# A Mamba layer and a mixture of experts on one core: softplus from exp and ln in one table set, every piece placed anew, both stages in one block

## The reference, cut to what matters

```python
xz = x @ in_proj_w.T + in_proj_b
x_in, z = jnp.split(xz, 2, axis=-1)                      # 512 channels each
x_conv = silu(conv over 4 taps of x_in + conv_b)
x_dbl = x_conv @ x_proj_w.T
dt_low, Bm, Cm = ...                                      # 64, 16 and 16 columns of x_dbl
dt = jax.nn.softplus(dt_low @ dt_proj_w.T + dt_proj_b)    # what the change computes in another way
A = -jnp.exp(A_log).T
# per token, channel d and state s:
A_bar = exp(dt * A);  h = A_bar * h + (A_bar - 1) / A * B * x;  y = sum_s h * C + D * x
y = y * silu(z);  out = y @ out_proj_w.T + out_proj_b
x = layernorm(x + out)
# then: sigmoid gate, top 2 of 16 experts, silu(x @ wg) * (x @ wu) @ wd for each, the shared expert,
# weighted sum, residual, layernorm
```

## Time and profile before

| what | value |
|---|---|
| median of 3 runs | 2208.38 us |
| the profiled execution, its own time | 2207.55 us |
| its span | 2205.7 us |
| TensorE busy in the span | 2053.2 us (93%) |
| VectorE busy | 1826.8 us (83%) |
| ScalarE busy | 1782.1 us (81%) |
| GpSimd busy | 1775.2 us (80%) |
| mean granted TensorE clock | 0.981 |

### The profile page before, as it was taken

The page is one execution under the profiler, slowest core; times in us unless marked ns, Lnnn a source line. Parts: engine busy times, 40 slices in busy tenths (PEclk is TensorE's granted clock), DMA queues, the critical chain, the costliest instruction groups (busy, mean ns, idle before and its releaser), DMA issues. The chain is left out here.

```text
span 2205.7 us, 68576 instructions
## 1 busy us (share of the span) xinstructions
PE 2053.2 (93%) x26550; PEld 1252.6 (57%) x26550; DVE 1826.8 (83%) x3055; ACT 1782.1 (81%) x3561; POOL 1775.2 (80%) x1699
## 2 busy tenths in 40 slices
PE   6899999999999999999999999999999897999996
PEld 2455555555555555555555555555555554889964
DVE  2898999989998989888989898889898995555556
ACT  4888888888888888898989897979898873677747
POOL 2787898979897989898989898889898985576654
PEclk9999999999999999999999999999999998999999
DMA  2232333333333233333232333233333355497668
GB/s 90 69 101 78 110 97 110 92 107 97 111 93 115 88 115 93 110 90 118 88 118 90 112 90 117 83 111 95 108 99 99 92 161 179 120 282 217 208 213 286
DMA packets 152304, 267.46 MB, mean 121 GB/s; under 512 B 26408, under 2 KB 65324, under 8 KB 151470
## 3 DMA queue, kind: packets, MB, share of 16 engines
q1 hardware_dynamic: 137198, 220.93, 33.2%
q0 software_dynamic: 14784, 42.16, 5.4%
HBM read 205.62 MB, written 57.39 MB: 119 GB/s over the span
## 5 line engine op out<-in xcount | busy, mean ns | idle before, releaser
L617 POOL TENSOR_TENSOR hc<-h,c_rep 128x512 f32<-128x512 f32 x1024 | 1284.9, 1276 | 208.7 <-DVE h L1175 167.1
L1175 DVE TENSOR_TENSOR_SCAN h<-g_ps,carry,h 128x512 f32<-128x512 f32 x1024 | 1273.9, 1272 | 71.7 <-ACT h L691 52.4
L691 ACT ACTIVATE h<-dt,a_mat 128x512 f32<-128x512 f32 x1024 | 694.9, 714 | 107.5 <-POOL hc L617 44.0
L969 PEld LDWEIGHTS g_ps<-b_steps,x_conv_rows 64*64 64x64 f32 x16384 | 477.8, 134 | 296.4 <-issue 207.3
L969 PE MATMUL g_ps<-b_steps,x_conv_rows 64*64 64x128 f32 x16384 | 560.3, 274 | 27.2 <-DVE h L1175 21.8
L930 PE MATMUL y_ps<-hc,dg_inv 64*64 64x512 f32 x2048 | 501.3, 604 | 13.6 <-DVE y_gated L1182 5.8
L931 PE MATMUL y_ps<-hc,dg_inv 64*64 64x512 f32 x2048 | 499.9, 604 | 0.0
L930 PEld LDWEIGHTS y_ps<-hc,dg_inv 64*64 64x64 f32 x2048 | 139.4, 135 | 231.7 <-issue 156.8
L1661 POOL DMA_INDIRECT y_planes<-gathered,home x144 | 139.7, 970 | 100.5 <-DVE gathered L2094 78.9
L1867 PE MATMUL banks<-gathered,w_now 128*128 128x128 f32 x1152 | 155.2, 278 | 4.0 <-ACT w_now L1729 3.4
L1867 PEld LDWEIGHTS banks<-gathered,w_now 128*128 128x128 f32 x1152 | 141.2, 193 | 6.6 <-issue 5.9
(11 more groups left out here) (275 smaller groups left out, 2864.1 us busy)
## 6 DMA issues: line engine op xcount, KB each, us to landing
c_rep<-bc_rows SPq DMA_DIRECT2D x512, 256.0 KB
gathered<-slot_rows SPq DMA_DIRECT2D x144, 129.5 KB, 3.5
gathered<-y_planes SPq DMA_DIRECT2D x32, 512.0 KB, 8.5
w_up<-in_x_t SPq DMA_DIRECT2D x16, 512.0 KB, 4.8
x_raw<-in_x_tok SPq DMA_DIRECT2D x16, 512.0 KB, 5.0
out<-x_t SPq DMA_DIRECT2D x16, 512.0 KB, 3.2
x_t_rows<-y_gated SPq DMA_DIRECT2D x15, 512.0 KB, 4.6
x_t<-x_t_rows POOLq DMA_DIRECT2D x12, 512.0 KB, 5.3
```

Source lines behind the costliest of these rows:

```text
L617: nc.gpsimd.tensor_tensor(hc[:, at_all % HCS], h[:, at_all % SLOTS], c_rep[:, at % CS], ALU.mult).then_inc(hc_ready, 1)
L691: nc.scalar.activation(h[:, (ITEMS * u + m) % SLOTS], dt[:, c], ACT.Exp, scale=a_mat[:, c, s:s + 1]).then_inc(factor_ready, 1)
L969: one = nc.tensor.matmul(g_ps[some, e, r * T + k * P:r * T + (k + 1) * P], x_rows[rows, c, k, some], steps_of, start=True, stop=True)
L1175: nc.vector.tensor_tensor_scan(slot, du, slot, carry[:, batch(u), c, s:s + 1], ALU.add, ALU.mult).then_inc(scanned, 1)
```

## The change

What it does, part by part:

1. **Softplus.** Sigmoid, Square, the factor pieces (a, b) and VectorE's products go. In their place stand one Exp (`take_exp`) and one Ln (`take_ln`) of 128x1024 per two chunks, in place. `preload_act_table_set` asks for the table set that holds both exp and ln, once ahead of everything and again right behind each Silu and each Sqrt.
2. **Places.** All tables have new numbers; `BY_SCALAR` has 5 members, where it had 4.
3. **First units.** Unit -1 and unit 0 get place tables of their own (`PLACE_FIRST`, `PLACE_SECOND`). In unit -1 each half's Silu comes by itself; two of the X pieces for unit 1 move from unit -1 into unit 0 (Y2, Y3); VectorE takes the other two.
4. **Loads.** The five small inputs are issued by ScalarE's queue; w_in comes in two halves, the half for z later.
5. **One block.** `moe` goes on in the same block; in place of the barrier each engine waits for what it needs (`mamba_left`, `weights_in`). Three tables that `moe` made with iota are made in unit 0 by GpSimd (`number_tiles`).

```diff
-LN2 = 0.6931471805599453
-ATANH = ((0.7285826631594803, 0.9233720476354889, 0.5983295270554391),
-         (0.7285826631594803, -0.561895576392733, 1.0626849249989152))
+EXP_AND_LN = "natural_log_exp_and_others"
-BY_SCALAR = (2, 4, 6, 7)
+BY_SCALAR = (1, 3, 4, 5, 6)
...
-        PLACE = [("x0", 1), ("d2", 1), ("d3", 1), ("x1", 2), ("T2", 4), ("x2", 4), ("c0", 6), ("c1", 6), ("a3", 11), ("T3", 13),
...
+        PLACE = [("x2", 0), ("T2", 1), ("d2", 2), ("d3", 2), ("c0", 6), ("c1", 6), ("x1", 8), ("x0", 9), ("T3", 11), ("z3", 11),
+                 ("o0", 11), ("o1", 14), ("z2", 19), ("z0", 20), ("z1", 20), ("r0", 22), ("r1", 22), ("c2", 26), ("c3", 26),
...
-        STEPS_AT = [52, 52, 59, 59, 63, 71, 78, 78]
-        SCATTER_AT = (1, 5, 6, 7, 12, 13, 14, 15)
-        ADD_RELU_AT = (60, 61, 22, 29)
+        STEPS_AT = [52, 52, 60, 61, 61, 75, 80, 85]
+        SCATTER_AT = (3, 7, 8, 9, 12, 13, 15, 19)
+        ADD_RELU_AT = (59, 60, 25, 26)
+        EXP_AT = (49, 15)
...
+        LN_AT = (50, 18)
...
+        LATER_BY = {'T0': 2, 'T3': 1, 'X2': 1, 'X3': 1, 'bc': 2, 'c0': 1, 'c1': 1, 'c2': 2, 'd0': 2, 'd1': 3, 'd2': 3, 'd3': 2, 'e': 1, 'lg': 1, 'low': 1, 'o0': 3, 'o1': 2, 'r0': 3, 'r1': 3, 'r2': 1, 'r3': 1, 't0': 2, 'x1': 1, 'x2': 1, 'x3': 4, 'z0': 2, 'z1': 2, 'z2': 1, 'z3': 4}
...
-        block = ctx.enter_context(nc.Block())
+        kept.block = block = kept.stack.enter_context(nc.Block())
...
-            for group, loaded in ((EARLY, early_in), (SMALL, small_in)):
-                for name in group:
-                    sp.dma_start(holders[name][:], d[name]).then_inc(loaded, 16)
+            sp.dma_start(w_in[:, :, 0:DI], d["w_in"][:, :, 0:DI]).then_inc(early_in, 16)
...
+            sp.dma_start(w_in[:, :, DI:], d["w_in"][:, :, DI:]).then_inc(later_in, 16)
...
             def add_relu(n, c):
 
-                emptied_all(pool, host("b", c, n), [f"b{c}"])
+                pool.wait_ge(ln_made, count(n, 2, c // 2 + 1))
                 nc.gpsimd.tensor_tensor(dt[:, c], dt[:, c], x_arg[:, c % 2], ALU.add).then_inc(dt_ready, 1)
...
         def _(act):
-            act.wait_ge(early_in, 16 * len(EARLY))
+            for name in SMALL:
+                nc.scalar.dma_start(holders[name][:], d[name]).then_inc(small_in, 16)
             act.wait_ge(zeroed, 7)
             act.wait_ge(small_in, 16 * len(SMALL))
+            nc.scalar.preload_act_table_set(EXP_AND_LN)
             nc.scalar.activation(a_mat[:], a_log[:], ACT.Exp).then_inc(a_exp, 1)
...
-            def find_z(n, g):
+            def take_exp(n, g):
 
                 act.wait_ge(abs_done, count(n, CH, 2 * g + 2))
-                nc.scalar.activation(x_arg[:], x_arg[:], ACT.Sigmoid, scale=-1.0, bias=shifts[:, 0:1]).then_inc(z_ready, 1)
-
-            def squared(n, g):
...
-                nc.scalar.activation(square[:], x_arg[:], ACT.Square).then_inc(square_ready, 1)
-
-            def factor(u, t):
...
-                nc.scalar.activation(work[:, bank], square[:, c % 2], ACT.Square, scale=root,
-                                     bias=shifts[:, k + 1:k + 2]).then_inc(filled[bank], 1)
+                nc.scalar.activation(x_arg[:], x_arg[:], ACT.Exp, scale=-1.0).then_inc(exp_made, 1)
+
+            def take_ln(n, g):
+
+                act.wait_ge(exp_made, count(n, 2, g + 1))
+                nc.scalar.activation(x_arg[:], x_arg[:], ACT.Ln, bias=1.0).then_inc(ln_made, 1)
 
             def root(pu):
                 act.wait_ge(norm_step, count(pu, NORM, 11))
                 nc.scalar.activation(spread, spread, ACT.Sqrt).then_inc(std_ready, 1)
+                nc.scalar.preload_act_table_set(EXP_AND_LN)
...
+                if u < 0 and m in SILU_FIRST:
+                    half = 2 * SILU_FIRST.index(m)
+                    emptied_all(act, u, [f"c{c}" for c in (half, half + 1)])
+                    two = x_conv[nq][:, half:half + 2]
+                    nc.scalar.activation(two, two, ACT.Silu).then_inc(x_conv_ready, 1)
+                    nc.scalar.preload_act_table_set(EXP_AND_LN)
...
-            def softplus(u, t):
...
-                nc.vector.scalar_tensor_tensor(out=x_arg[:, c % 2], in0=work[:, bank], scalar=ATANH[k][2], in1=x_arg[:, c % 2],
-                                               op0=ALU.add, op1=ALU.mult).then_inc(emptied[bank], 1)
...
-        block = ctx.enter_context(nc.Block())
+        block = kept.block
+
+        def mamba_left(eng):
+            eng.wait_ge(kept.gated, CH * UNITS)
+            eng.wait_ge(kept.carried, QUADS * UNITS - 1)
+            for q in range(2):
+                eng.wait_ge(kept.emptied[q], kept.in_work[q])
+
+        def weights_in(eng):
+            eng.wait_ge(kept.up_in, 16 * UP_LOADS)
+            eng.wait_ge(kept.down_in, 16 * LOADS)
```

230 lines of the change are left out of this document (129 added, 101 removed), and 6 rows, old and new, of the table PLACE.

## The result

The changed kernel takes 2186.61 us (median of 4 runs, 2183.79 to 2189.35), beside 2208.79 us of the kernel before on the same chip: ratio 0.9891, 95% interval 0.9871 to 0.9911. That is 22 us, not the 70.5 forecast, and outside the range. The profiled execution took 2189.35 us, with a span of 2187.5 and a mean granted clock of 0.979; the kernel before had a span of 2205.7, so the two traces differ by 18.2 us.

What follows compares the result with a forecast made beforehand. TensorE was taken as nearly the bound for three quarters of a unit, with ScalarE delaying it in the second stretch. Gains of 49.5 + 12 + 9 = 70.5 us from 2207.55 gave 2137, median 2138 us; range 2112 to 2160, chance 0.60.

Steps and rivals of the forecast that it cites:

- What was removed and added: Softplus and table loads, per steady unit: ScalarE 97.2 to 88.8 us, VectorE 6.4 less, TensorE and GpSimd unchanged.
- What a unit gains: Steady Mamba units: 3.3 us less each, 109.2 in place of 112.5; fifteen units give 49.5 us.
- the two waits of the earlier trace: TensorE's waits on ScalarE in items 0 to 15, 1.36 and 0.90 us: both go whole, 2.26 us per unit.
- The further 1.0 us from the other idle time: TensorE's other 2.5 us idle per unit: 1.0 goes, since banks no longer carry a and b pieces.
- what low clock costs: Steady units: 0.8 us per unit on average from TensorE's lower clock, part of the 5.6 us upper bound.
- The lead-in: Start of the Mamba stage, up to the first factor at 56.6 us: 12 us gained, ends 3 and 17.
- 43 as the place to look: Sign in the profile after: the first factor comes near 43 us.
- The change of blocks: Between Mamba and expert stages, where TensorE stood still 9.73 us: 9 us gained, bounds 5 to 9.7.
- the 2 named: Sign in the profile after: TensorE's idle time at the change of stages is under 2 us.
- Rival 1: Steady units: TensorE holds the pace, a unit gains only 1 us, 2172 us in all; chance 0.26.
- Rival 3: Slower: o1 waits for z3's bank, each missing item costing 1.76 us per unit; 2243 us; chance 0.03.
- The forecast's own signs: Wrong if a unit stays above 111.5 us, or TensorE shows new waits on banks around o and z pieces.

Runs made afterwards that it cites:

- e6: Changed kernel with the steady units' places, items and four BY_SCALAR members of the kernel before, keeping Exp and Ln; ratio 1.0008 to the kernel before.
- e4: Changed kernel plus 13 extra ScalarE copies of 128x512 in each of units 1 to 14; ratio 1.0100 to the kernel before.
- e17: Changed kernel without convolution taps 1 and 2 in units 1 to 14 (outputs differ from the reference); ratio 0.9860 to the kernel before.
- e18: Changed kernel with GpSimd's eight scatters per unit spread to items 3, 7, 10, 13, 16, 19, 21, 23; ratio 0.9881 to the kernel before.
- e14: Changed kernel with z3 copied at item 14, bc at item 46, d0 and d1 taken one item sooner; ratio 0.9780 to the kernel before.
- e5: Changed kernel with the Mamba and expert stages in two blocks again; ratio 0.9941 to the kernel before.
- e9: Changed kernel with X2 at item 47, between bc and lg, lg moved to 48, both copied one item earlier; ratio 1.0093 to the kernel before.
- e11: Changed kernel with the sixth step matrix (item 11) made by VectorE instead of ScalarE; ratio 0.9919 to the kernel before.

## Why the prediction was right or wrong

**What was removed and added: right.** ScalarE 88.8 us per unit, forecast 88.8; VectorE 6.4 less forecast, 101.4 to 96.0 measured, 5.4; 68 loads; Ln 1046 ns for my 1.1 us, Exp 1041 for 1148. The loads stand as costed, 1283 ns each; the group of fifteen shown above has 0.3 us of idle time before it in all. The drain of some 1380 ns that the Trainium skill, ScalarE: Activation LUTs, section What ACT_TABLE_LOAD costs, puts beside a load is in no row here.

**What a unit gains: wrong, and this is the step that failed.** 3.3 us were forecast, 49.5 in all. Measured: nothing in the unit's mean time, 0.6 us net, 0.95 between full-clock units. The sentence that failed is that the two waits of the earlier trace rows "lie in the stretch in which ScalarE is full; I let them go whole". e6 shows them at 1.38 and 0.91 us with ScalarE 10 us lighter, half of which it now waits for GpSimd. The row that I should have given weight to is in the same group: in that stretch GpSimd was busy 29.17 of 30.96 us. I quoted it and then cleared GpSimd by its mean over the unit, 98.7 of a possible 101, although I had cut the unit in stretches just to avoid such means. ScalarE's 29.95 us there were no sign that it alone set the pace. e4 (more ScalarE work, little longer) shows that for ScalarE's load, e17 (less TensorE work, same unit) for TensorE's, and e18 (scatters spread, some 1.5 us shorter) shows GpSimd behind the largest of the new waits, z3's. Behind the two waits of the earlier trace rows themselves it is not shown: their successors, 1.29 and 0.41 us, are the same in e18, and what would shorten them stays open. The further 1.0 us from the other idle time had no row behind it, and TensorE's idle time per full-clock unit is 5.17 us for 5.13.

**The clock: a term that I held fixed.** The forecast used what low clock costs only as part of an upper bound. Between the two profiled executions the low time rose from 30.6 to 47.7 us in the thirteen units, and by 7 in the tail: 12 us in all at half a us each, 13 for the units alone when counted against full-clock units, beside a gain of 18.2. That the change as such lowers the clock is not shown by this: over the whole span the four runs of the changed kernel that were measured beside seven of the kernel before have a mean granted clock of 0.977 to 0.981, and those 0.972 to 0.979. That the order around bc decides much of it, e14 shows in all its runs.

**The lead-in: sized somewhat low.** 12 forecast, in bounds of 3 to 17. The first factor comes at 44.67 instead of 56.58, 11.9 sooner, as worked out (I named 43 as the place to look). At item 48 of unit 1 the lead is 17.0: the further 5 us, between the first factor and there, were not in the sum. Up to 1.7 of them are low clock (10.3 us of it until there, 13.7 before); the rest would fit the places that units 0 and 1 now have, but no run parts it. They hang on the tables fitting together, since in e6 this stretch takes 22 us more.

**The change of blocks: right in kind.** TensorE's idle time is 1.41 us, under the 2 named, and its first eight matmuls no longer run at the lower level. Between the two traces it is 6.3 us, in e5 9.1 and by the ratios some 11; forecast 9. The gathers were not late next, as argued. What stands there after is VectorE's x_t (2.86 us) and the copied weights, as before.

**Rivals.** Rival 1 (a unit gains 1 us, 2172) came nearest: 0.95 us per full-clock unit, and the measured time lies in its range. Its reason, TensorE holding the pace, is not what the runs show: TensorE's work can shrink by 2.9 us without any gain, though it can't grow by 6.9 without a loss of 4.0. Rival 3 had the place right, z3's bank ahead of o1, and far too high a price: 1.65 us, about 1.0 of it real. The forecast's own signs said so: I had named a unit above 111.5 and new waits around the o and z pieces as what would prove me wrong, and both stand in the profile. With the terms as measured the sum is 7.4 for the units without the clock (13 x 0.57), 17.0 for all until item 48 of unit 1, 6.3 from the last gate product on, less 0.6 that the tail lost besides, less 12 for the clock: 18.1, beside the 18.2 us between the two traces. That this closes is no proof of the terms, since the same two traces give them.

## What to carry to other kernels

An engine that waits in short pieces for a second engine may in truth wait for a third, as TensorE did for z3's bank: before letting a wait go with the second engine's load, read what that engine's own queue waits for in the same stretch, and compare all engines' shares there, not over the period. Here lighter engines gave next to nothing by themselves; a copy three items sooner gave 1.0 us per unit and spread scatters some 1.5, where 10 us less of ScalarE's work had given 0.2 at most (e6). And where matmuls of few columns stand together, look at the granted clock there, in several periods and in several runs, ahead of any comparison: here the low time went from 3 to 106 us among kernels that do nearly the same work.

## What the hardware showed that I had not expected

- TensorE's clock fell while it was busy all the time, in runs of small matmuls (8 of 16 columns, two of 64, then 16 of 16 with a fill between), and in both kernels it stayed low for 3.4 or 6.8 us each time in the thirteen units (in e9 also 10.2 and 13.7). The same run of matmuls kept 2.4 GHz in other units of the same kernel. How many of the thirteen units are hit goes from none (e14) to all (e4, e11, e18), and no run here settles by what rule.
- Low time ran from 3.4 us (e14) to 105.7 (e4) between 230 and 1700 us, by which the clock cost some 2 to 53 us; e18 lost its whole gain to it.
- Exp and Ln of one table set followed each other with no load between, 1.04 and 1.05 us on 128x1024.
- The same program can take longer in the expert stage alone, and not by the chip: the last gate product of the changed kernel starts at 1832.98 and at 1833.82 us in its two profiled executions, and the spans are 2187.5 and 2221.4. The kernel before took 2250 and 2210 us on one and the same chip at different times. The cause is open.
